# Nine sets of transposes per sequence as row halves into pairs of score banks

## What is computed

```python
x = L0_attn_x                                   # (16, 512, 128)
xn = _layernorm(x, axis=-1)
x = x + _L0_attn_ref(xn, ...) + _L0_ffn_ref(xn, ...)   # 16 heads of 64, ALiBi, causal; FFN 128-512-128
xn = _layernorm(x, axis=-1)
x = x + _L1_attn_ref(xn, ...) + _L1_ffn_ref(xn, ...)   # 8 heads of 2 x 8, rotary, differential; FFN
```

## Time and profile before

| | us |
|---|---|
| median of 3 runs | 2450.73 (2449.71 to 2452.09) |
| profiled execution | 2447.2 |
| its span, first to last instruction | 2445.4 |
| PE busy | 2289.5 (94%) |
| DVE busy | 1850.2 (76%) |
| ACT busy | 1845.2 (75%) |
| POOL busy | 1452.2 (59%) |

### The profile page before, as it was taken

One profiled execution on the slowest core, in us unless ns is written; L12 is line 12 of the kernel. 1 busy time (PEld: TensorE's weight loads), 2 busy tenths in 40 slices (PEclk: granted clock), 3 DMA queues, 4 the chain that ended last, 5 costly groups with the idle time before them and its releaser, 6 DMA issues.

```text
span 2445.4 us, 87807 instructions
## 1 busy us (share of the span) xinstructions
PE 2289.5 (94%) x35968; PEld 1199.6 (49%) x35968; DVE 1850.2 (76%) x5125; ACT 1845.2 (75%) x4195; POOL 1452.2 (59%) x1356
## 2 busy tenths in 40 slices
PE   7999999999999999999999999999999999999777
PEld 3555455455545445555455545445555455545421
DVE  5568697887878778697887878778697887877674
ACT  5877777877777777777877778787777877777435
POOL 6976484756747566484756747566484756647211
PEclk9999999999999999999999999999999999999877
DMA  3020020200102020020200102020020200102020
GB/s 103 3 58 3 7 59 7 54 7 24 41 7 58 7 54 7 7 58 7 54 7 25 41 7 58 7 53 8 7 59 7 54 7 24 42 3 58 2 58 6
DMA packets 59967, 70.83 MB, mean 29 GB/s; under 512 B 11056, under 2 KB 55344, under 8 KB 56368
## 3 DMA queue, kind: packets, MB, share of 16 engines
q1 hardware_dynamic: 59568, 65.21, 11.1%
HBM read 35.04 MB, written 29.36 MB: 26 GB/s over the span
## 4 chain that ended last, share of the span: by engine, by line
PE 70%; DVE 11%; ACT 10%; issue 5%; DMA 2%; POOL 2%; SPq 0%; ACTq 0%; POOLq 0%; DVEq 0%
PE pj L1599 19%; PE pj L1725 9%; PE sc L1663 9%; PE pj L1695 9%; DVE mx L1366 6%; PE pj L1711 5%; PE pj L1619 5%; PE sc L1680 5%; ACT pt L1049 4%; PE sc L1758 4%; PE sc L1772 4%; ACT pq L999 3%; PE pj L1589 2%; POOL pq L848 1%; DVE pq L1313 1%
## 5 line engine op out<-in xcount | busy, mean ns | idle before, releaser
L848 POOL TENSOR_SCALAR pq<-pq,rsum 128x128 f32<-128x128 f32 (+3 forms) x1024 | 1157.2, 1145 | 496.7 <-DVE rsum L1320 496.7
L1366 DVE TENSOR_REDUCE mx<-sc 128x2 f32<-128x1024 f32 x512 | 616.0, 1218 | 159.7 <-PE sc L1772 156.2
L1049 ACT ACTIVATE pt<-sc 128x1024 f32<-128x1024 f32 x512 | 513.9, 1027 | 170.8 <-PE sc L1758 164.5
L999 ACT ACTIVATE pq<-pq,mx 128x128 f32<-128x128 f32 (+3 forms) x1024 | 567.4, 564 | 18.3 <-DVE mx L1313 17.2
L1313 DVE CUSTOM_DVE_ANT_0 pq<-sc,relkey 128x128 f32<-128x128 f32 (+3 forms) x1024 | 450.5, 484 | 165.8 <-PE sc L1663 164.2
L1017 ACT ACTIVATE pt<-sc 128x384 f32<-128x384 f32 (+1 forms) x768 | 361.6, 530 | 75.5 <-PE sc L1680 74.3
L1663 PE MATMUL sc<-K,Q 64*128 64x128 f32 (+3 forms) x2048 | 360.6, 450 | 2.8 <-ACT pt L1017 0.8
L1695 PE MATMUL pj<-pt,v 128*32 128x128 f32 (+2 forms) x7168 | 305.1, 321 | 0.4
L1680 PEld LDWEIGHTS sc<-ident,pq 64*128 64x128 f32 x5120 | 209.6, 139 | 109.5 <-issue 63.9
L1599 PE MATMUL pj<-xnT,wqkv 128*32 128x512 f32 x2048 | 254.9, 612 | 4.6 <-ACT xnT L950 2.0
L1695 PEld LDWEIGHTS pj<-pt,v 128*32 128x32 f32 x7168 | 202.4, 110 | 78.9 <-issue 49.2
(11 more groups left out here) (117 smaller groups left out, 2932.7 us busy)
## 6 DMA issues: line engine op xcount, KB each, us to landing
scr_p<-y SPq DMA_DIRECT2D x160, 128.0 KB, 3.5
QS<-scr_p SPq DMA_DIRECT2D x30, 384.0 KB, 5.6
KS<-scr_p SPq DMA_DIRECT2D x30, 384.0 KB, 5.7
x_in<-in_L_attn_x SPq DMA_DIRECT2D x16, 256.0 KB, 2.8
scr_p<-tanh SPq DMA_DIRECT2D x32, 128.0 KB, 3.4
out_x<-xres SPq DMA_DIRECT2D x15, 256.0 KB, 2.3
QS<-nrow SPq DMA_DIRECT2D x180, 4.0 KB
wqkv<-in_L_attn_w_qkv SPq DMA_DIRECT2D x1, 1536.0 KB, 6.8
```

Source lines behind the costliest of these rows:

```text
L848: pool.tensor_scalar(rows, rows, rsum[:, row_slot(i, p), c:c + 1], None, ALU.mult).then_inc(s_scl, 1)
L999: act.activation(rows, rows, ACT.Exp, scale=-1.0, bias=mx0[:, row_slot(i, p), c:c + 1], accum_out=lsum[:, row_slot(i, p), c:c + 1]).then_i ...
L1049: act.activation(pt1[:, slot:slot + 2, :], sc_pairs[both // 2][:, :, :], ACT.Exp, scale=float(DS) ** -0.25).then_inc(s_exp1, 2)
L1366: dve.reduce_max(mx1[:, g % 2, n:n + 2 * NT + 1:2 * NT], sc_pairs[both // 2][:, :, :], AXIS.X).then_inc(s_mxd1, 2)
```

## The change

All nine uses of `transpose4` become `transpose_halves`, which transposes the upper and lower 64 rows of each block separately, one half into each bank of a pair of score banks, as `turn_probs` does. The `pj` banks lose nine uses for each sequence, and the three score pairs gain nine. The readers take both banks of the pair in one instruction (ACT), or one half after the other (DVE's `head_norm_a`, which now has two reciprocals and two products). The three pairs of copies in `copy_turned` become three copies of two banks each. The load lists are reordered, the QKV weights are split in two loads, PE waits for the identity matrix alone and first does twelve transposes whose result nobody reads; the wait for `loads[0]` moves to the first projection. ACT does one small activation early. PE's first feed-forward product waits for `w1` alone. The order of steps on PE, ACT, DVE and POOL and many due ticks change; the last sequence's second attention is done in 25 ticks where it was 28.

```diff
-L1_TICKS = (28, 28)
+L1_TICKS = (28, 25)
-CLOCKS = (TICKS * NB + 6, (4, 4, 0), (2, 2, 0), (5, 0, 6), (17, 24, 30), (1, 35, 8))
+CLOCKS = (TICKS * NB + 6, (2, 4, 0), (2, 2, 0), (5, 0, 7), (18, 30, 29), (5, 33, 8))
-HT0_AT = 1
+HT0_AT = 0
-NA_LAG = (0, 4)
+NA_LAG = (0, 1)
...
-        loads = [[(ident[:, :], a["t_ident"]), (wqkv[:, :], a["L0_attn_w_qkv"]), (qscale[:, :], a["t_qscale"]),
-                  (relkey[:, :], a["t_relkey"])], [], []]
+        w_qk, w_v = slice(0, 2 * INNER), slice(2 * INNER, 3 * INNER)
+        loads = [[(wqkv[:, w_qk], a["L0_attn_w_qkv"][:, w_qk]), (qscale[:, :], a["t_qscale"]),
+                  (relkey[:, :], a["t_relkey"]), (wqkv[:, w_v], a["L0_attn_w_qkv"][:, w_v])], staged(0), []]
...
+                sp.dma_start(ident[:, :], a["t_ident"]).then_inc(s_id, 16)
...
         def _(act):
-            act.wait_ge(s_ld[0], NLOAD[0])
+            act.wait_ge(s_pset, 1)
+            act.activation(early[:, :], minus_half[:, 0:1], ACT.Copy)
...
-                to = pt[:, base + TURN_BASE[g]:base + TURN_BASE[g + 1]].rearrange("p (n h c) -> p n h c", h=2, c=HALF)
-                act.activation(to[:, :, h, :], sc[tile_bank(i, "tr0", m)][:, 0:cols].rearrange("p (n c) -> p n c", c=HALF),
-                               ACT.Copy).then_inc(s_ev, 1)
+                to = pt[:, base + TURN_BASE[g]:base + TURN_BASE[g + 1]].rearrange("p (n h c) -> p h n c", h=2, c=HALF)
+                act.activation(to, sc_pairs[both // 2][:, :, 0:cols].rearrange("p h (n c) -> p h n c", c=HALF),
+                               ACT.Copy).then_inc(s_ev, 2)
...
         def _(pe):
-            pe.wait_ge(s_ld[0], NLOAD[0])
+            pe.wait_ge(s_id, 16)
+            for _ in range(12):
+                pe.transpose(sc[SCB - 1][:, 0:P], ident[:, :], ident[:, :])
...
-            def transpose4(i, name, src):
-                t, full = bank(i, name)
+            def transpose_halves(i, kind, n, src):
+
+                for h in range(2):
+                    bank_free(i, kind, 2 * n + h)
                 for k in range(NT):
-                    last = pe.transpose(t[:, P * k:P * (k + 1)], src(k), ident[:, :])
-                last.then_inc(full, 1)
+                    for h in range(2):
+                        r = slice(HALF * h, HALF * (h + 1))
+                        last = pe.transpose(sc[tile_bank(i, kind, 2 * n + h)][:, HALF * k:HALF * (k + 1)], src(k)[r, :], ident[r, r])
+                        if k == NT - 1:
+                            last.then_inc(s_trf[kind], 1)
...
-                        pe.wait_ge(s_vprep, (N_VPREP0, N_VPREP)[l])
-                    b, u = pj_use(i, f"hT{l}")
-                    pe.wait_ge(s_pje[b], u)
+                        pe.wait_ge(s_vprep, (N_W1, N_VPREP)[l])
+                    pe.wait_ge(s_trc[f"hT{l}"], i.upto(2, 2))
```

Of the new PE order in steady state the part for the third tick of a pair shows the kind of move: the second attention's key scores and row-maxima scores now alternate, `others` (in which the transposes stand) comes earlier, and the widest scores of the first attention come at its end where they headed the fourth tick:

```diff
                 elif r == 2:
...
-                    second_values(h, k, 0)
                     p, i = pair(g, -1)
                     if i is not None:
                         project_v(i, p)
                     second_tops(h, k, 0)
+                    second_values(h, k, 0)
+                    second_values(h, k, 1)
+                    others(g, h, k)
+                    second_keys(h, k, 1)
                     second_tops(h, k, 1)
-                    second_values(h, k, 1)
-                    others(g, h, k)
-                    second_keys(h, k, 1)
+                    p, i = pair(g, 0)
+                    if i is not None:
+                        max_scores0(i, p, 3)
```

More of the change, by code:

```diff
@@ L282, in clocks @@
     return shown
+TURNED4 = {**{name: (name, 0) for name in ("xnT0", "hT0", "xnT1", "hT1", "oT")}, f"o{NG - 1}": ("o", NG - 1)}
 def pj_order():
@@ L293, in second @@
                 order.append((f"n{group}", i.lo))
-            if (group := l1_heads(i, t, TURN_AT[i.last()])) is not None:
-                order.append((f"o{group}", i.lo))
     def values(h, k, part):
@@ L309, in misc @@
     def misc(g, h, k):
-        order.extend((name, i.lo) for tick, name in FIRST_MISC if (i := at(g, tick)) is not None)
-        order.extend((name, i.lo) for tick, name in SECOND_MISC for i in second_at(h, k, tick))
+        order.extend((name, i.lo) for tick, name in FIRST_MISC if name not in TURNED4 and (i := at(g, tick)) is not None)
+        order.extend((name, i.lo) for tick, name in SECOND_MISC if name not in TURNED4 for i in second_at(h, k, tick))
     for g, h, k in clocks():
@@ L360, in pj_order @@
             values(h, k, 1)
+        elif late(g) and r == 2:
+            second(h, k, 0)
+            values(h, k, 0)
+            values(h, k, 1)
+            second(h, k, 1)
+            pairs("v", g, -1)
+            misc(g, h, k)
+        elif late(g) and r == 3:
+            second(h, k, 0)
+            values(h, k, 0)
+            values(h, k, 1)
+            misc(g, h, k)
+            second(h, k, 1)
+        elif r == 0:
+            pairs("q", g, -1)
+            pairs("k", g, -1)
+            values(h, k, 0)
+            values(h, k, 1)
+            misc(g, h, k)
+            second(h, k, 0)
+            second(h, k, 1)
+        elif r == 1:
+            second(h, k, 0)
+            pairs("pv", g, 3)
+            misc(g, h, k)
+            values(h, k, 0)
+            values(h, k, 1)
+            second(h, k, 1)
         elif r == 2:
@@ L385, in second_keys, with second_turns, misc @@
                 order.extend(("st1", 2 * (t - KEY_LAG[i.last()]) + n, i.lo) for n in range(2))
+    def second_turns(h, k, part):
+        for i, t in l1_steps(h, k, part):
+            if (group := l1_heads(i, t, TURN_AT[i.last()])) is not None:
+                order.extend(("o", 2 * group + n, i.lo) for n in range(2))
+    def misc(g, h, k):
+        for tick, name in FIRST_MISC:
+            if name in TURNED4 and (i := at(g, tick)) is not None:
+                kind, m = TURNED4[name]
+                order.extend((kind, 2 * m + n, i.lo) for n in range(2))
+        for tick, name in SECOND_MISC:
+            if name in TURNED4:
+                kind, m = TURNED4[name]
+                order.extend((kind, 2 * m + n, i.lo) for i in second_at(h, k, tick) for n in range(2))
     def second_tops(h, k, part):
@@ L884, in tick @@
                 if late(g) and r == 0:
-                    small(g, h, k)
-                    p, i = pair(g, 2)
-                    if i is not None:
-                        scale_probs(i, p, 3)
                     p, i = pair(g, 1)
@@ L969, in copy_q @@
             def copy_q(i, p):
+                if i.first() and p == 0:
+                    act.wait_ge(s_ld[0], NLOAD[0])
                 b, u = pj_use(i, f"q{p}")
@@ L1480, in tick @@
                         invert_sums(i, p, 2)
+                    p, i = pair(g, 1)
+                    if i is not None:
+                        invert_sums(i, p, 3)
                     second_attention(h, k, 0)
```

513 lines of the change are left out of this document (253 added, 260 removed).

## The result

The changed kernel takes 2464.25 us (median of four runs, 2460.74 to 2465.96) against 2450.22 (2449.66 to 2452.09) for the kernel before on the same chip: a ratio of 1.0057, 95% interval 1.0045 to 1.0069. I had forecast 2415, with 2387 to 2441 as the range. The profiled execution took 2460.74, its span is 2458.9.

The account below looks back on a forecast made before the run. PE was taken as the bound, idle 4% in the middle. Transposes -25, pairs and order 0, copies 0, start -6.5, end -2 sum to -33.5: from 2450.7 to 2417, leaned to 2415 us; range 2387 to 2441.

Parts of the forecast that it names:

- PE work removed: On PE, nine sets as row halves: 26.8 us less, plus 6.4 us of switches, 33 us in all.
- Score pairs: Nine more uses of the three score pairs a sequence: 0.03 us a set, 4 us; bounds 0 to 82 us.
- rival 1: Score pairs become the bound: 0.57 us wait a set, +40, 2491 us; decides from 0.29 us a set; chance 0.09.
- What reaches the end: Of PE's 33 us saved, a quarter stays in front of waits and 25 us arrive; bounds 16 to 33.
- The order: New order alternating key scores and row maxima: -4 us, cancelling 4 us of pair waits; bounds -16 to +16.
- Copies: ACT's two-bank copies save 1.6 us a sequence, off the path: sum 0, range -10 to +5 us.
- The start: Earlier first transposes, projection and feed-forward product, head start kept: 6.5 us gained, range 4.6 to 8.7.
- The end: Last sequence's second attention in 25 ticks, not 28: 2 us gained, bounds -10 to +10.
- The signs: Middle waits of L1758 and L1772 above 90 us: rival 1 or 2; below 60: rival 3; PE idle share 4%.
- Rival 2: Readers swallow the saving: DVE and ACT pace the second attention, PE only idles more; 2442 us; chance 0.07.
- rival 3: New order removes waits too: all 33 us arrive, PE idle falls 1 to 1.5 us a sequence; 2389; chance 0.24.
- Rival 4: Row halves don't run side by side: 0.5 us a set, +9 and the start gained, about 2451 us; chance 0.02.

Follow-up runs that it names:

- struct_only: Kernel before with only the nine sets as row halves in score pairs, old order, NA_LAG (0, 1): 2482.86 us, ratio 1.0133.
- all_but_struct: Changed kernel with the nine sets put back as full transposes in pj banks; new order, copies and start kept: 2454.3 us, ratio 1.0019.
- short readers: Second attention's row maximum and exponential cut to a quarter: before 2338.92 us, changed kernel 2355.82, struct_only 2346.65, all_but_struct 2346.18.
- full_in_pairs: struct_only with each set as four full transposes into the first bank of its pair, both banks held: 2498.09 us, ratio 1.0193.
- old_order: struct_only plus the two-bank copies and the new start, on the old order of steps: 2477.62 us, ratio 1.011.
- start_xn_h1: Kernel before with the new start and only xnT0, xnT1 and hT1 as row halves in score pairs, old order: 2445.98 us, ratio 0.9991.
- fill_xn_h1: start_xn_h1 plus nine idle transposes a sequence, one head pair ahead of the long wait: 2455.54 us, ratio 1.0025.
- fill_copies: Kernel before with new start, two-bank copies and nine idle transposes a sequence, one head pair ahead of the long wait: 2469.02 us, ratio 1.0078.

## Why the prediction was wrong

**What bounds the kernel.** Right: PE, with its waits at the score pairs. I also named the risk. The sum then gave it too little.

**PE work removed.** Too low for sets that nothing blocks. Such a set gives back 0.28 (`oT`) to 0.39 us (`xnT0`), by the fences above, where I had 0.19. (For the last instruction of a set I used 0.27 us; its mean in the earlier trace rows is 0.284, which makes the first term 24 us in place of 27.) The difference is the switch: I took projections (rows of form 128\*32) and full transposes (128\*128) for one kind. But `oT` saves 0.28, which is the 0.186 of the set and one switch of 0.10, although it stands behind a 128\*32 group as before. So that neighbour is a switch with either form, and the one toward the scores is gone. The kernel before shows it too: two groups of form 128\*32 overlap by 1196.90 + 1.08 - 1197.83 = 0.15 us, such a group and the transposes behind it by 1216.62 + 1.08 - 1217.64 = 0.06. Summed over the nine places with their neighbours, with nothing blocked, it is 2.8 us a sequence, an estimate of 45 us in all and not 33. Behind a wait the overlap is lost, so less of it shows: PE's busy time fell by 15 us in struct_only, by 23 from all_but_struct to the changed kernel, and by 30 and 33 with the short readers. This error was to the good side and makes the next one larger.

**Score pairs: the step that failed.** I took 0.03 us of added wait a set. The difference of two kernels that differ by the sets is what the pairs cost (waits, and overlap lost at them), less 45 us of work, plus what the mean clock took or gave (its difference times the span). The last column is PE's added idle time by the profiled executions alone, span less busy time, without the estimate of 45:

| | difference | clock's part | cost, for each of 144 sets | PE's added idle, for each |
|---|---|---|---|---|
| old order (struct_only against before) | +33 | +13 (0.981 to 0.976) | (33 + 45 - 13)/144 = 0.45 us | 55.3/144 = 0.38 us |
| new order (after against all_but_struct) | +9 | -8 (0.978 to 0.9815) | (9 + 45 + 8)/144 = 0.43 us | 33.7/144 = 0.23 us |
| old order, short readers | +7 | +2 (0.9915 to 0.991) | (7 + 45 - 2)/144 = 0.35 us | 36.1/144 = 0.25 us |
| new order, short readers | +12 | +2 (0.989 to 0.988) | (12 + 45 - 2)/144 = 0.38 us | 41.3/144 = 0.29 us |

So a set brings 0.23 to 0.38 us of idle time, and costs up to 0.45, against my 0.03. The clock's part has a check in the windows of 5 us: between 150 and 2150 us falls cost 5.1 us of work before and 15.3 in struct_only, 10.1 in all_but_struct and 1.7 in the changed kernel. My bounds, 0 to 0.57, held the price, and I chose the wrong end. The reason that I gave in rival 1 misled me: that 128 waits at 1568 uses mean that most uses meet a free pair. They do, because between two uses PE had enough other work; that says nothing on how much is to spare. What counts is a place's slack: how long the pair's last reader was done when PE came back to it. A set in the rotation makes every pair come back one use earlier, and a row-half set fills its pair in 0.25 us, about as fast as the second attention's scores do. I knew the order by heart for the switches and never laid the pairs beside it. Reading so would have shown it: `hT1` and `o3` are two uses between score group and transposed probabilities, and with three pairs that closes the circle.

**What reaches the end.** The quarter that I left in front of waits was the same mistake, smaller. full_in_pairs against struct_only shows it nearly alone: by the estimate 45 us of work went, and 14 us arrived, with DVE's head norm in more steps.

**The order.** I put -4 us on it, with bounds of 16 to either side. It costs 9 us without the sets (all_but_struct, where 4 or more are the clock's) and brings 13 with them (old_order against after), which is what the clock gives back there, 0.976 to 0.9815. The alternation did what I said, the DVE wait of row-maxima scores is gone. Not seen was that a projection for the second attention's rotary keys now waits for its `pj` bank behind the copy of `K`, 0.83 us in nearly every sequence.

**Copies.** Right. The forecasts 0.81 and 1.00 us for 768 and 1024 elements stand as 804 and 1020 ns on the changed kernel's ACT, and the time shows nothing:

```profile
L1084 ACT ACTIVATE pt<-sc 128x768 f32<-128x768 f32 x256 | 205.7, 804 | 74.1 <-PE sc L1738 74.1
...
L1084 ACT ACTIVATE pt<-sc 128x1024 f32<-128x1024 f32 x128 | 130.6, 1020 | 34.0 <-PE sc L1738 34.0
```

**The start.** Right in size where it stands alone, 6 us against 6.5. The changed kernel's timeline:

```profile
7.53 0.69 PE L1644 MATMUL sc<-ident,xn 64*128 64x64 f32 x8 [1.00 <-DVE xn L1322]
...
10.01 3.32 PE L1655 MATMUL pj<-xnT,wqkv 128*32 128x512 f32 x16 [1.79 <-DMA wqkv<-in_L_attn_w_qkv]
...
24.10 1.06 PE L1655 MATMUL pj<-hT,w 128*32 128x512 f32 x8 [0.57 <-DVE w L1273]
```

The projection starts at 10.0 (forecast 9.6) and the feed-forward product at 24.1 in place of 27.4. The sixteen matmuls still take 3.32 us, so the idle transposes saved at most 0.3 of the 2.5 that I had allowed. In the changed kernel the lead is 3.1 us at the second sequence's `xnT0` (83.1 against 86.2 us), short of the 4.6 that I took as the least, and gone by 186 us: the first long wait for `K` takes 2.3 us and one that the view puts down to issue 2.1. There "PE is bound, so the head start is kept" failed.

**The end.** 0 against my -2; no gain of the denser ticks shows, and no run has them alone.

**The signs.** I had written that waits of L1758 and L1772 above 90 us would speak for the pairs, and below 60 for a gain. They came out at 49, with a slower kernel. The two lines were only those that waited before. The right sign is the sum over every user of a pair, sets and transposed probabilities among them: about 78 us before, 104 after. The other sign, PE's idle share unchanged at 4%, was plainly broken: 6.2%. PE's busy time did fall by 26.5 us, near the 30 that I had named, and that said nothing about the end.

**The rivals.** Rival 1 was the mechanism, at less than its price: 0.43 for 0.57 by the table, 0.23 to 0.38 by the idle time. I gave it 0.09. Its decision point, 0.29 us a set, was worked out from 33 us of work and lies within that spread, so it decides nothing; what decides is that the sets cost 9 and 33 us net in the two orders. Rival 2, the saving swallowed, happened in start_xn_h1, but mostly by the clock and not by the readers. Of rival 3 one half came true: the order removed 18.7 us of waits, and brought others. Rival 4 is out: `hT1` takes 0.24 us from its start to that of `o3`, so the halves do run side by side.

**What was left out.** The clock, in every term. I read it as full in the middle, which is true to the tenth that the page shows, and it moves this kernel by up to 15 us.

## What to carry to other kernels

Work moved to a resource that is taken in turn must be checked place by place: who had this buffer one round ago, when is its reader done, and how much of the engine's own work stands between. The total of today's waits is no measure of that slack, and a faster fill shortens it. Look at every user of the resource for the new waits, not at those that waited before. And on an engine that is the bound, compare the mean clock too, and try to fill the longest wait with idle work of its length before you judge what a saving is worth: here three sets out of nine, the new start and seven idle transposes give 14 us where the whole change loses as much.

## What was not expected of the hardware

**The granted clock falls behind one wait, and where the wait was filled it stayed up.** A fall of the kernel before, shown in 5 us around it, and one of struct_only in its own 3.5 us (columns as in the earlier trace rows; the third number from the end is the clock):

```profile
875.00:880.00 5.00, 4.51 (x34) 1.39 (x36) 2.82 (x14) 4.97 (x10) 5.00 (x6) 0.66 0.01 2
```

```profile
885.50:889.00 3.50, 3.50 (x18) 0.54 (x16) 1.60 (x11) 3.50 (x8) 3.50 (x5) 0.51 0.03 7
```

And what PE did then, in struct_only:

```profile
883.15 0.59 PE L1740 MATMUL sc<-ident,pq 64*128 64x64 f32 x12 [0.40 <-ACT pt L1106]
883.55 0.57 PE L1818 MATMUL sc<-QS,KS 51*128 51x512 bf16 x2
885.30 0.41 PE L1818 MATMUL sc<-QS,KS 51*128 51x512 bf16 x2 [1.18 <-ACT pt L1106]
885.64 3.54 PE L1661 MATMUL pj<-xnT,wqkv 128*32 128x512 f32 x16
```

The group of sixteen takes 3.54 us there, against 1.92 at full clock (the `xnT0` fence above has one of the same size). A fall costs (1 - 0.66) x 5 = 1.7 us of work. In the changed kernel PE waits 0.66 us at this place in each sequence, and the one fall left in the stretch is behind its 2.3 us wait for `K`, at 165 us. all_but_struct has the same order and waits 0.96 us there in each of thirteen sequences; behind three of them the clock falls, as here:

```profile
875.00:880.00 5.00, 4.72 (x38) 1.91 (x40) 1.99 (x9) 5.00 (x10) 4.83 (x6) 0.66 0.01 2
```

So a wait can cost more than its length, and 0.96 us is enough for it here. Why the clock falls behind some waits of 0.96 or 1.16 us and not behind others of the same kernel isn't settled, nor why nine idle transposes some 20 us earlier kept it up in fill_xn_h1 and not in fill_copies.

**Column forms switch too.** That a 128\*32 projection next to a 128\*128 transpose pays the same 0.1 us as a row form does is the reason of the larger saving above. In the Trainium skill, TensorEngine Tiling (Array Packing), Key Properties, a change of tiling mode drains the engine; read literally, with columns counted as part of the mode, it would have told me, and the trace agrees with 0.28 us for `oT`.
